# A convolution and ConvLSTM kernel whose two-way scan is rebuilt: units of one direction with 512 columns, packed operand rows, GpSimd forming the rest of h

## The reference

```python
inp = jnp.concatenate([xr, h], axis=1)                  # 48 + 48 channels, one row of 32 columns
gates = conv_general_dilated(inp, w_mid, (1,), 'SAME')  # 3 taps along the row, 192 outputs, plus bias
i, f, g, o = jnp.split(gates, 4, axis=1)
c2 = sigmoid(f) * c + sigmoid(i) * tanh(g)
h2 = sigmoid(o) * tanh(c2)
```

## Time and profile before

| | |
|---|---|
| median of 3 runs | 726.75 us (725.79 to 728.73) |
| the profiled execution | 726.26 us, span 724.4 us |
| TensorE busy | 627.0 us (87%), 4532 matmuls |
| VectorE busy | 510.8 us (71%) |
| ScalarE busy | 547.2 us (76%) |
| GpSimd busy | 107.3 us (15%) |
| mean granted TensorE clock | 0.932 of full |

### The profile page before, as it was taken

One profiled execution on the slowest core, in us unless ns is written; L12 is line 12 of the kernel. 1 busy time (PEld: TensorE's weight loads), 2 busy tenths in 40 slices (PEclk: granted clock), 3 DMA queues, 4 the chain that ended last, 5 costly groups with the idle time before them and its releaser, 6 DMA issues.

```text
span 724.4 us, 16291 instructions
## 1 busy us (share of the span) xinstructions
PE 627.0 (87%) x4532; PEld 461.4 (64%) x4532; DVE 510.8 (71%) x1169; ACT 547.2 (76%) x1059; POOL 107.3 (15%) x98
## 2 busy tenths in 40 slices
PE   5975843999999999999866999999999999999930
PEld 1223522555555555555526999999999998888910
DVE  2678760899999999999884666666666666666635
ACT  3731550788888888888864999999999888888845
POOL 2500310133222222233232000000000000300000
PEclk9986885999999999999987999999999999999965
DMA  9956699555555566556420000000001221176216
GB/s 213 270 158 176 164 113 109 126 125 129 128 130 133 135 138 135 128 124 130 101 59 20 23 22 22 22 22 22 22 22 45 63 64 46 57 153 139 74 54 174
DMA packets 102890, 72.22 MB, mean 100 GB/s; under 512 B 54799, under 2 KB 90129, under 8 KB 102145
## 3 DMA queue, kind: packets, MB, share of 16 engines
q1 hardware_dynamic: 102096, 68.25, 41.2%
q10 hardware_dynamic: 768, 3.67, 2.1%
HBM read 47.37 MB, written 22.35 MB: 96 GB/s over the span
## 4 chain that ended last, share of the span: by engine, by line
PE 69%; DMA 9%; ACT 8%; issue 6%; DVE 5%; SPq 2%; POOL 1%; DVEq 0%; ACTq 0%
PE pz L662 39%; PE pz L577 14%; PE p_out L585 4%; DMA y_hl<-y_d 4%; ACT gel L759 3%; DMA y_d<-y 3%; PE p_edge L538 3%; PE p_keys L525 2%; PE p_edge L673 2%; ACT selfg L753 2%; PE p_edge L540 2%; DVE hmax L1068 1%; ACT ab_lo L745 1%; DVE y_sb L1231 1%; SPq L281 1%
## 5 line engine op out<-in xcount | busy, mean ns | idle before, releaser
L1068 DVE TENSOR_REDUCE hmax<-gel 96x128 f32<-96x1024 f32 x128 | 154.3, 1206 | 48.4 <-ACT gel L759 47.9
L759 ACT ACTIVATE gel<-pz 96x1024 f32<-96x1024 f32 x128 | 130.7, 1023 | 72.2 <-PE pz L577 70.6
L662 PE MATMUL pz<-xh_hi,wl_hi 112*112 (+1 forms) x768 | 140.1, 291 | 5.5 <-POOL xh_lo L966 5.5
L662 PE MATMUL pz<-xh_hi,wl_lo 112*112 (+1 forms) x768 | 135.4, 285 | 0.0
L662 PE MATMUL pz<-xh_lo,wl_hi 112*112 (+1 forms) x768 | 135.2, 285 | 0.0
L662 PEld LDWEIGHTS pz<-xh_hi,wl_hi 112*112 112x112 f32 x768 | 107.7, 176 | 21.7 <-issue 8.4
L662 PEld LDWEIGHTS pz<-xh_hi,wl_lo 112*112 112x112 f32 x768 | 107.9, 177 | 0.0
L662 PEld LDWEIGHTS pz<-xh_lo,wl_hi 112*112 112x112 f32 x768 | 107.8, 177 | 0.0
L1168 DVE SCALAR_TENSOR_TENSOR h<-to,tc 48x256 f32<-48x256 f32 x128 | 53.7, 419 | 35.4 <-ACT tc L845 33.4
L1174 DVE TENSOR_TENSOR xh_lo<-h,xh_hi 48x256 f32 (+1 forms) x124 | 48.3, 416 | 33.3 <-ACT xh_hi L856 33.3
L966 POOL TENSOR_TENSOR xh_lo<-kl,xh_hi 48x512 f32 (+1 forms) x32 | 38.0, 1188 | 186.9 <-DVE idx L1044 96.6
(11 more groups left out here) (115 smaller groups left out, 947.5 us busy)
## 6 DMA issues: line engine op xcount, KB each, us to landing
ib<-idx_d SPq DMA_DIRECT2D x64, 256.0 KB, 4.3
y_d<-y SPq DMA_DIRECT2D x32, 192.0 KB, 3.4
y_hl<-y_d SPq DMA_DIRECT2D x32, 192.0 KB, 4.4
hist_d<-h SPq DMA_DIRECT2D x128, 48.0 KB, 1.6
hp<-hist_d SPq DMA_DIRECT2D x32, 192.0 KB, 2.6
kr<-xn_d SPq DMA_DIRECT2D x32, 98.0 KB
xn_d<-x_in SPq DMA_DIRECT2D x32, 96.0 KB, 2.2
kl<-xn_d SPq DMA_DIRECT2D x32, 96.0 KB
```

Of the source, the lines that this page charges most:

```text
L662: mm = pe.matmul(o, wgt[0:TOP, d, m, t], rhs, start=(n == 0), stop=(n == 8))
L759: act.activation(gel[:, t % 2], pz[0:O, 2 * (t % 2):2 * (t % 2) + 2, :], ACT.Gelu) \
L1068: dve.tensor_reduce(dst, gel[:, t % 2].rearrange("p w (r c k) -> p w r c k", r=WS, k=KN), AX_X, ALU.max).then_inc(S["maxed"], 1)
```

## The change

- **Row buffers.** `xh_hi` and `xh_lo` become one buffer `xh`. Its rows 0:48 hold the rest of x1, rows 64:112 its high part, and rows 48:64 and 112:128 copies ("twins") of high-part rows, made by two DMAs per row and direction, two steps ahead. A buffer `ht` (128 rows) holds the high part of h (0:48), ones (48:64), the rest of h (64:112), and a third copied piece of x (112:128, one DMA per unit); `he` holds the high part of h again in 64:112. `fill_rows` is gone.
- **Units.** A unit is now one direction d with all 512 columns. It has six matmuls of 128 rows on `xh` (`x_part`, which may run before h is known), three pairs on row halves (`ht` rows 0:48 for gates i,f and `he` rows 64:112 for g,o, with the rest of the weights `w_e`), and six of 128 rows on `ht`. TensorE's order is h_part(s,0), x_part(s,1), h_part(s,1), x_part(s+1,0).
- **ScalarE.** Two tanh of 96x512 from PSUM per unit, one of the cell on 48 rows, and the copy of h to `he` (`h_edge`).
- **VectorE.** `cu`, `cv`, the cell and h as before, each 48x512, once per unit; no rest of h.
- **GpSimd.** For each unit a cast of h into `ht` (`h_top`) and a subtraction for the rest (`h_lo`), 48x512 each. The memset of x1r moves behind the first step's. The scan's weights are scaled and split here, in five pieces in the last five groups' turns; SyncE loads them by 11 DMAs at group 26 and moves four blocks of `wl_rest` by DMA before the scan.

The core of the diff:

```diff
-            def fill_rows():
-                ...
+            def move_scan_weights():
+                sp.wait_ge(S["wl_split"], 4)
+                for k, first, n in ((0, C, HALF - C), (0, TOP, P - TOP), (1, C + 1, 1), (1, TOP, P - TOP)):
+                    sp.dma_start(w_xh[first:first + n, k].bitcast(F32), wl_rest[first:first + n, k].bitcast(F32)) \
+                        .then_inc(S["wl_moved"], 16)
+            def load_twins(s, d, b):
+                row = row_of(s, d)
+                for first, src in ((C, HALF), (TOP, HALF + 16)):
+                    sp.dma_start(xh[first:first + 16, reg(row, 0, 1), 0:SLOT - 1].bitcast(F32), ...)
+            def load_third(s, d):
+                if later(s):
+                    sp.wait_ge(S["gates"], s * 4 + (2 * d - 2))
+                ...
+                sp.dma_start(ht[TOP:P, d, 0:SLOT - 1].bitcast(F32), src.bitcast(F32)) \
+                    .then_inc(S[f"x_third{d}"], 16)
...
+            def x_part(s, d, b, n=None):
+                ...
+                for m in range(2):
+                    for t in range(TAPS):
+                        pe.matmul(pz[0:TOP, 2 * d + m, :], w_xh[:, 0, d, m, t], rhs, start=(t == 0), stop=False)
+            def h_part(s, d):
+                if later(s):
+                    pe.wait_ge(S["h_top"], s * 2 + (d - 1))
+                    pe.wait_ge(S["h_edge"], s * 2 + (d - 1))
+                for t in range(TAPS):
+                    for m, src in ((0, ht), (1, he)):
+                        rows = slice(HALF * m, HALF * m + C)
+                        pe.matmul(pz[0:TOP, 2 * d + m, :], w_e[rows, d, m, t], moving(src, rows, t),
+                                  start=False, stop=False)
+                if later(s):
+                    pe.wait_ge(S["h_lo"], s * 2 + (d - 1))
+                pe.wait_ge(S[f"x_third{d}"], s * 16 + 16)
+                for m in range(2):
+                    for t in range(TAPS):
+                        mm = pe.matmul(pz[0:TOP, 2 * d + m, :], w_xh[:, 1, d, m, t], moving(ht, slice(0, P), t),
+                                       start=False, stop=(t == TAPS - 1))
+                    mm.then_inc(S["gates"], 1)
...
+            def h_parts(s, d):
+                pool.wait_ge(S["h2_ready"], s * 2 + (d + 1))
+                passed(pool, "pool_passed")
+                pool.tensor_copy(h_slots(ht, 0, d), h2[0:C, d].rearrange("p (b w) -> p b w", w=W)) \
+                    .then_inc(S["h_top"], 1)
+                pool.wait_ge(S["h_top"], s * 2 + (d + 1))
+                pool.tensor_tensor(h_slots(ht, HALF, d), h2[0:C, d].rearrange("p (b w) -> p b w", w=W),
+                                   h_slots(ht, 0, d).bitcast(F32), ALU.subtract).then_inc(S["h_lo"], 1)
...
+            def cell(s, d):
+                ...
+                dve.scalar_tensor_tensor(cu[HALF:TOP, d], tif[HALF:TOP, d], 1.0, c2[HALF:TOP, d], ALU.add, ALU.mult)
+                ...
+                dve.scalar_tensor_tensor(cv[HALF:TOP, d], tif[0:C, d], 1.0, tgo[0:C, d], ALU.add, ALU.mult)
+                ...
+                dve.scalar_tensor_tensor(c2[HALF:TOP, d], cu[HALF:TOP, d], 0.5, cv[HALF:TOP, d], ALU.mult, ALU.add)
+                ...
+                dve.scalar_tensor_tensor(h2[0:C, d], tgo[HALF:TOP, d], 1.0, tc[HALF:TOP, d], ALU.add, ALU.mult)
```

More of the change, by code:

```diff
@@ L402, in turn @@
                     load_scan_weights()
-                if isinstance(j, int) and nth(j, b, 0)[0] == 1:
-                    fill_rows()
+                if isinstance(j, int) and nth(j, b, 0)[0] == GROUPS - 2:
+                    for s in range(2):
+                        load_twins(s, 0, s)
+                    sp.wait_ge(S["pads_set"], 9)
+                    load_third(0, 0)
                 for k, stage in ((3, load_y), (0, load_xres), (3, store_idx), (-2, store_x1), (5, load_keys),
@@ L411, in _ @@
             store_x1(GROUPS - 2, 0, GROUPS // 2 - 1)
+            move_scan_weights()
+            sp.wait_ge(S["x1_hi"], GROUPS)
+            for s in range(2):
+                load_twins(s, 1, s)
+            load_third(0, 1)
             store_x1(GROUPS - 1, 1, GROUPS // 2 - 1)
@@ L439, in step @@
             def step(s, b):
-                for x in range(2):
-                    store_h(s, x)
+                for d in range(2):
+                    if not isinstance(s, int) or s + 1 < H:
+                        load_third(s + 1, d)
+                    if isinstance(s, int) and s + 2 < H // 2:
+                        load_twins(s + 2, d, b)
+                    store_h(s, d)
                 if later(s, H // 2 + 1):
@@ L445, in _ @@
             step(0, 0)
[L446 removed]
+            with sp.Fori(0, H // 4 - 2) as j:
                 for b in range(2):
[L448 to L450 removed]
+                    s = j * 2 + (1 + b)
+                    for d in range(2):
+                        load_third(s + 1, d)
+                        load_twins(s + 2, d, 1 - b)
+                        store_h(s, d)
+            for s in range(13, 18):
+                step(s, s % 2)
             with sp.Fori(0, H // 4 - 4) as j:
@@ L633, in _ @@
             fc2(GROUPS - 1, 1, GROUPS // 2 - 1)
[L637 to L642, removed]
-                for m in range(2):
[L644 to L663, removed]
@@ L693, in _ @@
                 for b in range(2):
-                    for x in range(2):
-                        gates(j * 2 + (18 + b), x)
+                    s = j * 2 + (18 + b)
+                    h_part(s, 0)
+                    x_part(s, 1, b)
+                    h_part(s, 1)
+                    x_part(s + 1, 0, 1 - b)
                     project(j * 2 + b, b, j)
@@ L1106, in turn @@
                 self_max(*now)
-                if last:
-                    for part in range(3):
-                        scan_weights(part)
             for c in range(10):
@@ L1181, in step @@
             def step(s, projects=False):
-                for x in range(2):
-                    cell(s, x, last=isinstance(s, int) and s == H - 1)
-                    if x == 1 and projects:
+                for d in range(2):
+                    cell(s, d)
+                    if d == 1 and projects:
                         stats(s - (H // 2 + 3))
```

322 lines of the change are left out of this document (169 added, 153 removed).

## The result

The changed kernel takes **737.79 us** (median of 4 runs, 734.34 to 742.45) against 726.27 us (725.79 to 728.73) for the kernel before: a ratio of 1.0159, with a 95% interval of 1.013 to 1.0189. It is 1.6% slower. The forecast was 715 us, faster than before; the result lies just outside the range of 686 to 737.

A forecast was written before the change was run, and what follows sets the result against it. It took TensorE to bound the scan, and ScalarE and VectorE's gelu and maximum chain the edge stage, with a DMA-made hole. 726.26 - 23.4 + 1.3 + 10.5 = 714.7, median 715 us; range 686 to 737.

The forecast's parts named there:

- Part 1: Edge stage, about 100 to 120 us: without fill_rows the stall goes, -23.4 us (bounds 18 to 24).
- Part 2: Last groups and start of the scan: weight loading, scaling and splitting moved to GpSimd, together +1.3 us.
- Part 3: One scan step: VectorE and GpSimd exclude each other on SBUF reads; 4.73 us per unit, 9.46 per step.
- The seam: Scan start: first matmul waits for four wl_rest moves behind GpSimd's last piece, at 385 us against 385.87 before.
- TensorE's 3.45 us per unit: Scan: whole matmuls and pairs take 6.9 us per step instead of 8.8; 3.45 of a unit's 4.73, off the chain.
- The scan's sum: Whole scan: start, 37 units at 4.73, 13 steps at 9.95, memset 3; 316.4 us against 305.9, +10.5.
- A: Scan: no exclusion for scalar_tensor_tensor; 7.2 us a step, 8.3 with statistics; 655 us in all; chance 0.06.
- B: Scan: exclusion holds, but VectorE keeps or releases the port more cheaply; units 4.0 to 4.5, 675 to 700 us; chance 0.12.
- C: Scan: exclusion costs more; unit 5.33 us and 753 in all, or 4.96 and 729; chance 0.14.
- D: Scan: TensorE's clock falls in its gaps, units 6.9 us instead of 4.73; 748 us with 15 such; chance 0.08.
- E: Scan: the pairs do not run together; hidden, still 715 us; counted within the forecast, no chance of its own.
- a sign of being wrong altogether: Scan: granted clock leaving 1.00, or a twin or third-copy DMA ending TensorE's waits; no size given.

The follow-up runs named there:

- Experiment 6: Kernel before the change, constant rows set by GpSimd memsets instead of the two fill_rows DMAs, scan untouched: 704.74 us, ratio 0.973.
- experiment 1: Changed kernel, the eleven weight loads issued one per turn in groups 2 to 12 instead of all at group 26: 727.22 us, ratio 1.0019.
- experiment 2: Changed kernel, loads as in experiment 1 and GpSimd's weight pieces cut to fifteen smaller ones in groups 14 to 28: 719.15 us, ratio 0.9908.
- experiment 4: Changed kernel, tanh of i,f, cv and the cell's tanh in PSUM, so no VectorE cell operation has two SBUF inputs: 700.36 us, ratio 0.9668.
- experiment 3: Changed kernel, GpSimd's memset of x1r moved ahead of the first step's h parts: 733.47 us, ratio 1.0108.
- Experiment 7: Changed kernel with the edits of experiment 2 and experiment 3 together: 713.44 us, ratio 0.9818.
- experiment 9: Changed kernel with the edits of experiment 2, experiment 3 and experiment 4, pairs replaced by six single matmuls, no wait for h_edge: 709.98 us, ratio 0.9773.

## Why the prediction was wrong

Against its 714.7 us for the profiled execution, 734.34 were measured, 19.6 more. By its steps:

- **Part 1 (-23.4): right.** The distance behind the fills fell by 32.05 - 8.60 = 23.45; up to group 26 it is 24.7 with the neighbouring distances. Experiment 6 shows the same gain without any other part of the change (21.9, with memsets in its place).
- **Part 2 (+1.3): the step that failed**, by 15.4 us; measured are 20.1 - 3.4 = +16.7.
  - *The eleven weight loads* were put at nothing: they "delay SyncE one turn in which the one-hot concerned is two groups off". The prediction looked at the one-hot and not at the load of y that stands behind them in the same turn. That load was issued 5.5 us later and landed after 10.9 us instead of 4.4. It cost 11.2 us by the distances of experiment 1, 10.6 by the medians. The queue's own rows of before had the counterexample: the fills there were cheap to issue (0.69 and 0.63), and the y load behind them paid.
  - *The pieces on GpSimd* were sized at 5.5 us together: 3.5 for the last and 2 for the earlier ones, out of bounds of 0 to 5. Without the burst they are 8.9 by the distances, 4.9 for the earlier and 4.0 for the last (experiment 2: 8.1 back, by the medians). The rule for them was in the prediction's own part 3: one VectorE operation waits for the whole GpSimd operation. It was worked out for the last piece alone.
  - *The seam* was nearly right: the first scan matmul stands 4.63 behind the last piece (373.19 to 377.82), where 3.65 was forecast for the four moves, so 1.0 more.
  - The three misses, 11.2 + 3.4 + 1.0, are 15.6. The prediction's own terms of part 2 give +1.1 (2 for the pieces, 385 against 385.87) where it wrote +1.3; that is the rest.
- **Part 3, the mechanism: right.** That VectorE and GpSimd exclude each other and that this bounds the scan is shown by experiment 4. Of the terms of the chain, cast 0.47, `cv` 0.54, subtraction 1.04 and `c` 0.55 behind the other's end were forecast to 0.01. The unit was 4.73 by the sum and 4.80 measured: every second h waits 0.89 instead of 0.69 for the cell's tanh, and why is open.
- **TensorE's 3.45 us per unit: wrong, without effect on the time.** It is 3.92: six matmuls take 1.51, and three pairs 0.90. Inside a group the pairs do start 0.23 to 0.25 apart; what the sum left out comes with the changes of group. This is one part of the error of experiment 4's expectation.
- **The scan's sum (+10.5): right in sign, 6.5 too small.** Plain steps 9.60 instead of 9.46, steps that project 10.04 and more instead of 9.95, the memset 4.3 to 5.7 instead of 3 (experiments 3 and 7), the first h at 9.4 instead of 9.0.
- **Rivals.** A is dead (`cv` and `c` stand at 1.00 and 1.55). B and C are not it: the unit lies 0.07 from the forecast. D is not it in plain steps: there the granted clock is 1.00 (from 428 to 500 us). E, the pairs do run together, and experiment 9 sizes what they are worth. None of the rivals had its place ahead of the scan; the miss was in edits that had been put down as hidden.
- **Signs.** Two things that the prediction had called a sign of being wrong altogether did come, for short: the granted clock left 1.00, to 0.72 from 398 to 408 behind the memset's stop and to 0.91 from 640 to 660, and TensorE waited three times, 4.4 us in all, for the third copy of x, each time behind 640 us. Neither touches the plain steps. The first is part of the memset's price.

Experiment 7 puts it in one number: with the loads, the pieces and the memset out of the way, the changed scan gives 713.44.

## What to carry to other kernels

A block of loads put into an ordered queue delays the next load behind it twice, here by its own issues (5.5 us) and on the DMA engines (6.5 us), and what counts is who waits for that load; spread the block over turns in which the DMA share leaves room. When work moves to GpSimd, give its VectorE partner an input in PSUM, or count every operation of the pair as serial; here this alone was worth 37 us, and it decides whether cheaper matmuls pay at all. A change made of several parts is to be costed against each part done alone: the part that gained here needed none of the others.

## What the runs showed of the hardware

- The waiting engine of a VectorE and GpSimd pair ends 0.54 to 0.55 us (0.69 alone), 0.47 (cast, 0.60 alone) or 1.04 (subtraction, 1.18 alone) behind the other: some 0.14 us of its length is covered by the wait. In the unit shown (482.98 to 488.57) they take turns: `cu`, cast, `cv`, subtraction, `c`.
- A GpSimd memset does hold up VectorE's one-hot, which has a single SBUF input (tensor_scalar, 0.74 us for 1,024 elements). In experiment 6:

```profile
103.56 1.86 POOL L962 MEMSET xh_hi<- 32x2120 f32 x1 [0.61 <-DVE hmax L1078]
104.75 1.22 DVE L1071 TENSOR_SCALAR onehot<-ib,jcol_sb 128x1024 fp32r<-128x1024 uint16 x1
```

  It ends 0.55 after the memset. The memset of x1r beside scalar_tensor_tensor with two SBUF inputs stays at 6.92, and the VectorE operations at 0.69.
- VectorE's four operations of experiment 4 have two inputs each, and having one of them in PSUM makes no difference to their own time (0.69 and 0.70).
- A group of six matmuls of 512 columns takes 1.51 us, 0.25 each, and a group of three pairs on row halves 0.90, 0.30 a pair; the gathers' pairs start 0.23 apart.
- Where TensorE stood still for 4.84 us (398.13 to 402.97), its granted clock was 0.72 in the stretch 398 to 408, and six matmuls took 2.70 us instead of 1.51.
